# A chunked recurrence on one core: from chunks of 16 steps in two groups of rows to chunks of 32 steps in one group

## What is computed

```
xn = layernorm(x)
O_lh, O_rh = polar_orthogonal(W_lh), polar_orthogonal(W_rh)    # 12 iterations X <- 1.5 X - 0.5 X X' X
q = xn Wq',  v = xn Wv'
h = identity                                                  # state of each sequence, 128 channels
for t in range(512):  h = rms(h O_lh' + q[t] O_rh');  qs[t] = h
attn = (qs * v) Wc'
ffn = sqrt((xn cos(theta + theta_noise))^2 + (xn sin(phi + phi_noise))^2)
out = x + attn + ffn
```

## Time and profile before

| what | value |
|---|---|
| median of 3 runs | 178.69 us (177.2 to 179.84) |
| the profiled execution's own time | 178.86 us |
| its span, first to last instruction | 176.8 us |
| busy: PE, DVE, ACT, POOL | 83%, 70%, 57%, 31% |
| mean granted TensorE clock | 0.829 |
| DMA, mean | 28 GB/s |

### The profile page before, as it was taken

The page is one execution under the profiler, slowest core; times in us unless marked ns, Lnnn a source line. Parts: engine busy times, 40 slices in busy tenths (PEclk is TensorE's granted clock), DMA queues, the critical chain, the costliest instruction groups (busy, mean ns, idle before and its releaser), DMA issues.

```text
span 176.8 us, 2963 instructions
## 1 busy us (share of the span) xinstructions
PE 146.9 (83%) x726; PEld 114.7 (65%) x726; DVE 123.0 (70%) x561; ACT 99.9 (57%) x400; POOL 54.6 (31%) x91
## 2 busy tenths in 40 slices
PE   7988877699997699898499999656999999899840
PEld 7767766587876486576376666436777777677620
DVE  2599998126899689999779999933555555555640
ACT  3148999755776468778467687662444444333200
POOL 7007768000000013534235345334333333233300
PEclk9999999879999999999999999995555555555555
DMA  4950000000000000000000000000003003002210
GB/s 102 285 223 0 4 2 0 0 0 4 2 0 0 0 4 2 2 0 0 0 4 2 0 2 0 2 0 6 0 0 119 0 0 119 2 27 92 63 59 9
DMA packets 3492, 5.01 MB, mean 28 GB/s; under 512 B 464, under 2 KB 1616, under 8 KB 3472
## 3 DMA queue, kind: packets, MB, share of 16 engines
q1 hardware_dynamic: 3168, 4.46, 8.0%
q0 software_dynamic: 160, 0.26, 0.4%
q10 hardware_dynamic: 144, 0.07, 0.1%
HBM read 2.69 MB, written 2.10 MB: 27 GB/s over the span
## 4 chain that ended last, share of the span: by engine, by line
PE 56%; DVE 24%; issue 9%; ACT 5%; POOL 2%; DVEq 2%; POOLq 0%; ACTq 0%
PE bank L872 22%; DVE WT L607 7%; PE bank L839 4%; DVE WMID L626 4%; DVE SQM L629 4%; PE bank L827 4%; PE bank L817 3%; PE bank L848 3%; PE bank L778 3%; PE bank L764 3%; PE bank L874 3%; PE bank L733 2%; PE bank L830 2%; PE bank L758 1%; DVE PXT L561 1%
## 5 line engine op out<-in xcount | busy, mean ns | idle before, releaser
L391 ACT ACTIVATE SQE<-W 128x129 f32<-128x129 f32 x74 | 23.1, 312 | 41.3 <-DVE W L666 28.6
L872 PE MATMUL bank<-PXT,WT 128*128 128x128 f32 x136 | 41.1, 393 | 5.8 <-DVE WT L607 3.6
L872 PEld LDWEIGHTS bank<-PXT,WT 128*128 128x128 f32 x136 | 26.3, 240 | 23.4 <-DVE WT L607 21.8
L298 POOL TENSOR_TENSOR FS<-FSQ 128x256 f32<-128x256 f32 x16 | 11.6, 727 | 63.3 <-ACT FSQ L412 63.3
L666 DVE SCALAR_TENSOR_TENSOR W<-UZ,RT,bank 128x129 f32<-128x129 f32 x30 | 10.5, 351 | 21.0 <-PE bank L872 21.0
L817 PE MATMUL bank<-IDENT,W 128*128 128x128 f32 x68 | 24.9, 366 | 0.2 <-DVE W L645 0.2
L319 POOL TENSOR_TENSOR PV<-VT,WT 128x128 f32<-128x128 f32 x32 | 14.5, 454 | 31.7 <-DVE WT L607 31.7
L859 PE MATMUL bank<-WCT,PV 128*128 128x128 f32 x64 | 20.6, 427 | 1.8 <-POOL PV L319 1.8
L607 DVE COPY WT<-bank 128x128 f32<-128x128 f32 x70 | 19.9, 284 | 0.1
L859 PEld LDWEIGHTS bank<-WCT,PV 128*128 128x128 f32 x64 | 17.3, 331 | 2.5 <-issue 1.9
L839 PE MATMUL bank<-CS,XNT 128*128 128x256 f32 x64 | 18.8, 380 | 0.0
(11 more groups left out here) (131 smaller groups left out, 267.7 us busy)
## 6 DMA issues: line engine op xcount, KB each, us to landing
X<-in_L_attn_x_dram SPq DMA_DIRECT2D x8, 256.0 KB, 5.7
out_dram<-OUT SPq DMA_DIRECT2D x6, 256.0 KB, 2.8
out_dram<-OUT SPq DMA_DIRECT2D x4, 128.0 KB, 2.0
WP<-in_L_attn_W_rh_dram ACTq DMA_DIRECT2D x1, 64.0 KB, 2.0
WP<-in_L_attn_W_lh_dram SPq DMA_DIRECT2D x1, 64.0 KB, 2.3
ANG<-in_L_ffn_theta_dram POOLq DMA_DIRECT2D x1, 64.0 KB, 4.2
WV<-in_L_attn_Wv_dram SPq DMA_DIRECT2D x1, 64.0 KB, 3.9
ANG<-in_L_ffn_phi_dram POOLq DMA_DIRECT2D x1, 64.0 KB, 3.9
```

The costliest lines, as they stand in the source:

```text
L391: act.activation(SQE[:, 0:E], state(s, g)[:, 0:E], ACT.Square, accum_out=SSE[:, g:g + 1]).then_inc(ss_ready[g], 1)
L872: pe.matmul(Y[g][:, 0:P], stationary(m, g), OT[0][:, :], start=True, stop=True).then_inc(y1_done[g], 1)
```

## The change

Chunks have 32 steps, so that 8 x 16 = 128 chunks fill one group of rows, and there is no second group. Pass 0 starts at step 25 (3 moves), pass 1 is whole (16 moves) and is the last guess, and the final pass has 16 moves of two steps each: 35 moves of one group. In the final pass the middle state is needed for the output too: ACT takes its square sum (in place of DVE), PE transposes it into bank TM, DVE copies it to WTM. The start states of a pass are no longer normalised with their own end norm but scaled with the norm of the state before the last move (`end_prepared`, with the diagonal matrix made by POOL); the remaining ratio of norms, REND, is moved one row on by a one-column matmul with a shifting matrix, and RSTART scales u in the first step of the next pass. The check at the end is relative and uses the same scaling. Fill work is laid out anew per move, in a place A (behind the two matmuls, before the transpose) and a place B (behind the transpose). Two small constants are made during the polar iterations (`place_shift`, `place_e0`). Loads, layernorm, polar iterations, the preparation and the branch at the end are otherwise as they were. The core of the diff:

```diff
-STEPS = 16
-FIRST = 5
-GUESS_PASSES = 3
+STEPS = 32
+FIRST = 25
+GUESS_PASSES = 2
...
-    STORES = ((0, 4), (4, 8), (8, 12), (12, 14), (14, 16))
+    STORES = (4, 8, 12, 16, 20, 24, 28, 30, 32)
...
+    PAIRS = [*range(FIRST_PAIR + 1, STEPS // 2), *range(FIRST_PAIR + 1)]
...
+    PAIRS_A = {0: (1, 2, 3), 1: (5, 6), 2: (8, 9)}
+    PAIRS_B = {0: (4,), 1: (7,), 2: (10,), 3: (11,), 4: (12,), 5: (13,), 6: (14,), 7: (15,)}
+    FFN_A = {m: m - 3 for m in range(3, 3 + STEPS // 2)}
+    V_A = {10: 2, 11: 4, 12: 6, 13: 8, 14: 10}
+    V_B = {8: 0, 9: 1, 10: 3, 11: 5, 12: 7, 13: 9, 14: 11, 15: 12, 16: 13, 17: 14, 18: 15}
+    assert GUESSES == 19
...  (POOL)
+            def end_scaled(e):
+                pool.wait_ge(einv_ready, e + 1)
+                pool.tensor_scalar(DIAG[:, :], IDENT[:, :], EINV[:, 0:1], None, ALU.mult).then_inc(diag_ready, 1)
...  (ACT; root_of_state, where s ends a pass)
+                act.activation(REND[:, :], SSE[:, s % 2:s % 2 + 1], ACT.Sqrt,
+                               scale=EINV2[:, 0:1]).then_inc(rend_ready, 1)
+                act.wait_ge(shifted, e + 1)
+                act.activation(RSTART[:, :], FILL[:, P:P + 1], ACT.Identity,
+                               bias=E0COL[:, 0:1]).then_inc(r_ready, 1)
...  (ACT, each move)
+                if m < GUESSES:
+                    act.wait_ge(ssm_ready, m + 1)
+                else:
+                    act.wait_ge(mid_ready, m + 1)
+                    act.activation(SQM[:, 0:E], WMID[:, 0:E], ACT.Square, accum_out=SSM[:, 0:1]).then_inc(ssm_ready, 1)
+                    act.wait_ge(ssm_ready, m + 1)
+                act.activation(RT[:, j:j + 1], SSM[:, 0:1], ACT.Sqrt, scale=1.0 / C).then_inc(rm_ready, 1)
+                norm_of_state(m + 1)
+                for i in (*PAIRS_A.get(m, ()), *PAIRS_B.get(m, ())):
+                    pair_copied(i)
+                if m in FFN_A:
+                    ffn_squared(FFN_A[m])
+                if m - 1 in FFN_A:
+                    ffn_root(FFN_A[m - 1])
+                for i in (V_A.get(m, 0), V_B.get(m, 0)):
+                    if i % 2:
+                        v_copied(i // 2)
...  (DVE)
+            for m in range(GUESSES):
+                j = MOVES[m][0]
+                mid(m, j)
+                mid_norm(m)
+                second(m, j)
+                if ends_pass(m + 1):
+                    end_prepared(m)
+                end(m, j)
+                transposed(m + 1)
+            for m in range(GUESSES, LAST):
+                mid(m, j)
+                second(m, j)
+                mid_transposed(m, j)
+                end(m, j)
+                if j:
+                    written(j - 1)
+                if m + 1 < LAST:
+                    transposed(m + 1)
...
+                inverses(m, j)
+                written(j)
...  (PE)
+            transposed(0)
+            pair(0)
+            for m in range(LAST):
+                j = MOVES[m][0]
+                pe.wait_ge(wt_ready, m + 1)
+                pe.matmul(YB[:, 0:P], stationary(m), OT[0][:, :], start=True, stop=True).then_inc(y1_done, 1)
+                pe.matmul(PB[:, 0:P], stationary(m), O2T[:, :], start=True, stop=True).then_inc(y2_done, 1)
+                for i in PAIRS_A.get(m, ()):
+                    pair(i)
+                if m in FFN_A:
+                    ffn(FFN_A[m])
+                if m in V_A:
+                    values(V_A[m])
+                if m >= GUESSES:
+                    if j:
+                        projected(j - 1)
...
+                    pe.wait_ge(mid_ready, m + 1)
+                    pe.transpose(TM[:, 0:P], WMID[:, 0:P], IDENT[:, :]).then_inc(tm_done, 1)
+                transposed(m + 1)
+                for i in PAIRS_B.get(m, ()):
+                    pair(i)
+                if m in V_B:
+                    values(V_B[m])
+                if m >= GUESSES:
+                    projected(j)
```

More of the change, by code:

```diff
@@ L113, in bass_layer @@
-        WT = [[sb(f"WT{g}_{i}", [P, P]) for i in range(2)] for g in range(GROUPS)]
-        EDGE = [[sb(f"EDGE{g}_{i}", [P, GB, NCHUNK]) for i in range(2)] for g in range(GROUPS)]
-        DIAG = [sb(f"DIAG{g}", [P, P]) for g in range(GROUPS)]
+        X = sb("X", [P, STEPS, C])
+        XN = sb("XN", [P, STEPS, C])
+        XF = sb("XF", [P, STEPS, C])
+        OUT = sb("OUT", [P, STEPS, C])
+        XNT = sb("XNT", [P, STEPS * P])
+        VT = sb("VT", [P, STEPS * P])
+        UZ = sb("UZ", [P, STEPS // 2 * 3, PITCH])
@@ L116, in bass_layer @@
+        W = sb("W", [P, PITCH])
+        WMID = sb("WMID", [P, PITCH])
+        WT = [sb(f"WT{i}", [P, P]) for i in range(2)]
+        WTM = [sb(f"WTM{i}", [P, P]) for i in range(2)]
+        EDGE = [sb(f"EDGE{i}", [P, B, NCHUNK]) for i in range(2)]
+        DIAG = sb("DIAG", [P, P])
         SQE = sb("SQE", [P, PITCH])
         SQM = sb("SQM", [P, PITCH])
-        SSE = sb("SSE", [P, GROUPS])
-        SSM = sb("SSM", [P, GROUPS])
-        RM = sb("RM", [P, GROUPS])
-        RT = sb("RT", [P, TILES])
@@ L266, in further_passes, with redone @@
             with eng.If(more > 0):
+                starts()
                 with eng.Fori(1, NCHUNK) as p:
-                    for t in range(TILES):
-                        one_pass(p, t, *divmod(t, GROUPS))
+                    for j in range(STEPS):
+                        one_step(p, j)
             eng.end_ifs()
-        def redone(p, t):
-            return p * TILES + (t - TILES)
+        def redone(p, j):
+            return p * STEPS + (j - STEPS)
         @block.gpsimd
@@ new lines, in mid_norm, with second @@
+            def mid_norm(m):
+                dve.wait_ge(mid_ready, m + 1)
+                dve.tensor_tensor_reduce(out=SQM[:, 0:E], in0=WMID[:, 0:E], in1=WMID[:, 0:E], scale=1.0,
+                                         scalar=0.0, op0=ALU.mult, op1=ALU.add,
+                                         accum_out=SSM[:, 0:1]).then_inc(ssm_ready, 1)
+            def second(m, j):
+                dve.wait_ge(y2_done, m + 1)
+                dve.scalar_tensor_tensor(out=PB[:, 0:P], in0=UZ[:, uz(j) + 1, 0:P], scalar=norm_of(m),
+                                         in1=PB[:, 0:P], op0=ALU.mult, op1=ALU.add).then_inc(pre_ready, 1)
@@ L797, in _ @@
             pe.wait_ge(S["mt_copied"], 1)
-            for g in range(GROUPS):
-                last = pe.matmul(FB[0][:, g * P:(g + 1) * P], XNT[:, cols(FIRST, g)], MNT[:, 0, :], start=True, stop=True)
-            last.then_inc(S["u_first"], 1)
+            pe.wait_ge(S["xt_copied"], FIRST // BT + 1)
+            pe.matmul(FB[0][:, 0:P], XNT[:, tile(FIRST)], MNT[:, 0, :], start=True, stop=True).then_inc(S["u_first"], 1)
             for b in range(POLAR_ITERS - LN_ITER - 4, BATCHES):
```

628 lines of the change are left out of this document (280 added, 348 removed).

## The result

The changed kernel takes 159.37 us (median of four runs, 159.32 to 160.82); the kernel before took 177.94 us on the same chip (four runs). The ratio is 0.896, with a 95% interval of 0.887 to 0.906. The forecast was 162, with 154 to 172 as its range. The profiled execution took 159.34 us with a span of 157.5, so 1.84 us lie outside the span. Executions of one and the same kernel are spread over some 1 to 3%, the longer ones mostly at a lower mean clock, so a difference of medians under about 1% says nothing by itself.

A forecast was written before the change was run, and what follows sets the result against it. Bound by one group's chain latency: move 3's WMID at 52.3, 16 x 2.88 and 0.8 to 99.2, 15 x 3.29 to 148.6, W at 149.7, tail 10.4, span 160.1, 2.06 outside: 162 us. Range 154 to 172.

The forecast's parts named there:

- first WMID: Start of the moves: one pair ahead of the first move instead of four, WMID at 38.9 us instead of 40.99.
- first three moves: Moves 0 to 2: three rounds of 2.76 us plus 5.1 us for bank waits behind ACT's copies and the boundary.
- first final move, above the others: Start of the final pass: no wait beyond the usual 3.29 us round; the boundary ahead of it costs 0.8 us.
- start of the flag to the end: Tail: flag 5.4 us behind the last W, end at 10.4, nearly all of it a stretch without work.
- The round: One guess-pass move at full clock: seven latencies along the chain sum to 2.76 us, or 2.88 with the longer SQM.
- long SQM: Guess moves from the fourth on: SQM takes 416 ns instead of 295 where a POOL operation is under way.
- rival (3): Chain longer: no place B cover, ACT late, or POOL holding SQM; 172 us, 167 with SQM alone; chance 0.15 for both.
- Hidden, just: Place B in guess moves: a pair and the transpose need 0.75 us of PE and fit the gap of 0.77.
- Half clock in the final pass: Final pass: PE's thin work keeps the clock at half, round 3.29 us; chance 0.66, with 159 to 166 us.
- signs of being wrong: Fill-move pitch above 3.2 us, fill on the chain between W and L872, or the clock falling before 99 us.
- Rival (1): Final pass: the clock stays full, 0.44 us less a round, 155 us in all; chance 0.12.
- Rival (4): First boundary: clock falls and stays down, moves 3 to 18 take 64.5 us instead of 46.1, total 182; chance 0.05.

The follow-up runs named there:

- experiment 4: The changed kernel with each ffn matmul issued twice on PE in 16 guess moves: 167.57 us.
- experiment 3: The changed kernel with ACT copying pairs 1, 2, 5 and 8 ahead of the norm of the same move instead of behind it: 157.51 us.
- experiment 1: The changed kernel with dummy matmuls on PE in the final pass, into a bank that nobody reads: 154.5 us.
- 2: The changed kernel with the ffn work one move earlier and SIZE behind the fourth PV on POOL: 158.88 us.
- 12: The kernel of experiment 2 with the last four values matmuls placed earlier, none left in the boundary move: 157.81 us.
- 8: The changed kernel with 128 more instructions (fulfilled waits) on PE ahead of its first matmul: 177.5 us, one run; only the end is read.
- 9: The combined kernel of experiment 7 with the skipped further passes taken out of every engine's program: 146.49 us, 0.824 of the kernel before.
- 10: The combined kernel of experiment 7 with 120 more instructions (fulfilled waits) on PE ahead of its first matmul: 159.51 us, one run; only the end is read.
- 11: The combined kernel of experiment 7 with 64 wider dummy calls instead of 98, so PE's branch is instruction 1586: 148.74 us.
- experiment 6: The kernel before with dummy matmuls on PE in its final pass, projections over three banks instead of four: 169.23 us, 0.950 of the kernel before.
- experiment 5: The changed kernel with a third guess pass, 16 more moves without fill and one more boundary: 212.71 us, 1.196 of the kernel before.
- 7: The changed kernel with final-pass dummies, early ACT copies, ffn earlier, SIZE later and the last four values earlier: 149.68 us, 0.841 of the kernel before.

## Why the prediction was right

The mechanism was the forecast one: a single group bound by the latency of its chain, at full clock in the guess passes and at half in the final pass. In spans, 160.1 was forecast and 157.5 measured. That the total is so near is partly luck: the steps are off by 9.8 us in all, signs left out, and the two largest cancel. By the steps of the forecast:

| step | forecast | measured | difference |
|---|---|---|---|
| first WMID | 38.9 | 37.27 | -1.6 |
| first three moves | 13.4 | 12.95 | -0.4 |
| 16 guess moves with their boundary | 46.9 | 45.89 | -1.0 |
| first final move, above the others | 0 | 2.49 | +2.5 |
| 15 final moves at their pitch | 49.4 | 50.5 | +1.2 |
| last WMID to the flag | 6.5 | 6.2 | -0.3 |
| start of the flag to the end | 5.0 | 2.2 | -2.8 |

*The round.* "2.76", and 2.88 with a long SQM, were forecast; 2.81 is the commonest. The sum of seven ways, read from a kernel in which two groups overlapped, was right to 0.05 us, the single ways to 0.07. The transpose to its copy is 0.37, nearer to the low end of its bounds than to the 0.44 taken. The addition to W is 0.42, 0.04 more: ACT's root is late by that, which the forecast had as hidden. In the final pass the round is 3.37 instead of 3.29, mostly the way from the WT copy to L896 (0.42 instead of 0.34): the projection of the middle state, L888, stands between them on PE.

*SQM and POOL.* The forecast took the long SQM, 416 ns; with POOL under way it is 331 here; 0.08 us in each move is the 1.0 us of the third row. This is a matter of timing. In the fourteen profiles 145 SQM on DVE are longer than 0.30 us, and every one of them ends 0.14 to 0.16 us behind the end of a POOL addition (FS or XF) that was under way when it started. In the earlier trace rows they start up to 0.27 ahead of that end, in the changed kernel 0.18, in experiment 4 up to 0.71. SQM reads two operands from SBUF, and POOL's addition reads SBUF too. The Trainium skill (SBUF — State Buffer, "SBUF: two separate sides") says that two such operations exclude each other for a whole instruction. The traces agree, and the price reaches 0.56 us (0.85 instead of 0.29, experiment 4). The second half of rival (3) was therefore sound as a mechanism. It didn't come because in this layout the addition FS starts 0.54 ahead of SQM, and XF, 0.15 behind SQM's start, is the one that waits (0.77 instead of 0.72). Nothing in the forecast says so: this was luck too.

*Cover.* "Hidden, just" for place B and hidden for place A: yes; experiment 4 gives the room left, about 0.3 us in place A with ffn and values, 0.4 by the forecast (1.9 less 0.21 and 1.3). Rival (3), a longer chain, came only in small: the sixth to the eighth move are 2.90 to 2.91, because ACT's root of the middle norm stands behind its FR, ends at 59.74 in the seventh, and W starts at 59.84 after DVE had been idle for 0.20. That is 0.1 us in three moves, where the rival had 0.3 in 32.

*First moves.* 4.7, 3.9 and 4.9 against 4.51, 3.74 and 4.70; experiment 3 shows that the copies behind the norm are 2.3 of the 4.7 us above three plain rounds. Of the 1.6 us by which they begin earlier, 0.85 is there when the preparation begins (the matmuls L793 of the kernel before and L819 of the changed one start at 32.06 and 31.21). It begins early: four matmuls on ones from 4.5 us on take 0.64 us in the changed kernel's profile and 1.06 before, though the clock row reads 1.00 in both. In other profiles of the same code the first WMID stands at 36.6 to 38.9.

*The clock.* Half clock in the final pass, as forecast, and on the right ground: with dummies that give PE more to do the clock stays at 1.00 (experiment 1). One of the prediction's own signs of being wrong came in its letter, a fall of the clock before 99 us: it fell at about 96.7 (0.81 from 96.6 to 96.8, 0.50 behind). But the final pass had begun by then, at 96.11 instead of the forecast 99.2, and the guess moves had run at 1.00. Rival (1) put its price at 0.44 a round; experiment 1 measures 0.50. Rival (4), a fall at the first boundary that lasts, didn't come.

*What the forecast lacked.* Two terms that cancel. First, the wait of the projections was worked out for a move in the middle of the pass; for the first one POOL's queue had to be followed back, with what is queued ahead of PV(0): the last XF and SIZE. It costs 2.49 us, and is gone in experiments 2 and 12. Second, the stretch behind the flag was carried over as 5.0 us, as if it belonged to the end of a program; in the changed kernel and those made from it, it depends on where the code lies (experiments 8 to 11). 2.8 us of the 18.6 that the change gains in the comparison are this stretch, in which no engine works. What makes it long in the kernel before isn't shown.

*What the gain is.* Clock held and stretch alike, 169.2 to 154.5: 14.7 us from 74 slots of 1.6 and 1.2 us (1.2 in the final pass of experiment 6, 1.5 at half clock) giving way to 35 moves of 2.8 to 2.9, with the stall of the first final move still in it.

## What to carry to other kernels

When interleaved groups give way to a single one, the forecast is a sum of latencies: read each where the receiving engine was idle, and then treat the first round of each stage by itself, following every engine's queue back past the stage's border. Fill beside a latency chain isn't only free, it can hold the clock: moves without it were longer (3.22 us at half clock against 2.81 with fill). But look at what the fill's operations on other engines do to the chain's: a POOL addition that started just ahead of a DVE operation on the chain held it for 0.56 us. And a difference of 3 us behind the last instruction may be nothing but the place of a branch (experiments 8, 10 and 11), so look there before crediting a change with it.

## What the runs showed of the hardware

The stretch behind the flag takes 1.7, 2.0 to 2.1, or 4.6 to 5.4 us, and in the changed kernel and the eleven made from it, it goes by how many blocks of 256 instructions lie between PE's branch and what it jumps to (counted from the start of PE's program):

| kernel | branch, target | blocks ahead | behind the flag |
|---|---|---|---|
| 9 | 1716, 1719 | 0 | 1.7 |
| changed, 2, 3, 12 | 1330, 1696 | 1 | 2.0 to 2.1 |
| 11 | 1586, 1952 | 1 | 2.1 |
| 10 | 1842, 2208 | 1 | 2.1 |
| 4, 8 | 1458, 1824 | 2 | 5.3, 5.1 |
| 5 | 1498, 1864 | 2 | 5.4 |
| 7 | 1722, 2088 | 2 | 4.6 |
| 1 | 1750, 2116 | 2 | 5.0 |
| before | 1562, 1929 | 1 | 4.9 |
| 6 | 1859, 2226 | 1 | 5.2 |

The Trainium skill (Runtime: NRT & Kernel Launch, "Instruction fetch mechanics") says that engines refill their code in such blocks, two of them at hand, and that a taken branch to anywhere else waits for the fetch. The changed kernel and the eleven made from it agree, with 2.5 to 3.4 us as the price of the second block. The kernel before and experiment 6 don't, so on them it is not PE's branch. The other engines skip the same passes; ACT's jump crosses a block in the kernel before (443 to 576) and not in the changed one (354 to 487), but that wasn't tried. It crosses one in experiment 5 too (421 to 554), so that row isn't a clean case for PE. DVE's jump is the other way round: it crosses a block in the changed kernel (616 to 818), where the stretch is short, and not in the kernel before (809 to 1011).

A DVE operation with two operands in SBUF (SQM, 0.29 us by itself) that starts while a POOL addition is under way ends 0.14 to 0.16 us behind that addition's end (in all 145 cases in which it is longer than 0.30 us), and so takes up to 0.85 us (experiment 4). The other way round, a POOL addition of 0.73 us that starts within SQM takes 0.77 to 0.85.

A fulfilled wait isn't free on PE: 256 of them moved the first WMID by 15.3 us and 240 of them by 10.9 us, which is 60 and 45 ns each if all of the shift is theirs (without them it varies by 2.2 us among the profiles).
